# A five-hop graph kernel: first tile multiplied whole in fp32, two pieces of x and the visits of the last hop moved

## What is computed

```python
h = relu(A @ (x @ W1) + b1)
h = relu(A @ (h @ W2) + b2)
x = layernorm(x + h)
f1 = A @ x @ V1
f2 = A @ A @ x @ V2
f3 = A @ A @ A @ x @ V3
out = layernorm(x + (f1 + f2 + f3) / 3.0)
```

## Time and profile before

| | |
|---|---|
| time, median of 3 runs | 254.26 (253.55, 254.26, 254.32) |
| the profiled execution's own time | 253.49 |
| its span (first to last instruction) | 251.7 |
| PE busy | 244.9, 97% of the span |
| DVE busy | 203.2, 81% |
| ACT busy | 192.8, 77% |
| POOL busy | 16.0, 6% |
| chain that ended last | PE 84%, DVE 5%, ACT 3%, issue 3%, DMA 2% |
| split pieces of the ring | 240 on ACT at 629 ns, 240 on DVE at 687 ns |

### The profile page before, as it was taken

The page is one execution under the profiler, slowest core; times in us unless marked ns, Lnnn a source line. Parts: engine busy times, 40 slices in busy tenths (PEclk is TensorE's granted clock), DMA queues, the critical chain, the costliest instruction groups (busy, mean ns, idle before and its releaser), DMA issues.

```text
span 251.7 us, 3740 instructions
## 1 busy us (share of the span) xinstructions
PE 244.9 (97%) x1136; PEld 203.0 (81%) x1136; DVE 203.2 (81%) x395; ACT 192.8 (77%) x335; POOL 16.0 (6%) x23
## 2 busy tenths in 40 slices
PE   8999999999999999999999999999999999999991
PEld 8688888888888888886888888888888888888871
DVE  0998889896789889897888979767676767798865
ACT  2999899886868787978878787777777777779850
POOL 1000000000003021130000000000000000011322
PEclk9999999999999999999999999999999999999999
DMA  6999999930000000000043210000000000301002
GB/s 219 384 390 383 386 386 387 392 133 0 0 3 3 0 0 3 0 0 1 19 105 48 59 25 3 0 0 1 4 0 0 0 0 3 83 1 42 21 24 83
DMA packets 20276, 22.59 MB, mean 90 GB/s; under 512 B 9760, under 2 KB 10656, under 8 KB 20128
## 3 DMA queue, kind: packets, MB, share of 16 engines
q1 hardware_dynamic: 19968, 22.03, 25.5%
q10 hardware_dynamic: 288, 0.33, 0.4%
HBM read 20.25 MB, written 2.10 MB: 89 GB/s over the span
## 4 chain that ended last, share of the span: by engine, by line
PE 84%; DVE 5%; ACT 3%; issue 3%; DMA 2%; SPq 1%; POOL 1%; POOLq 0%; DVEq 0%; ACTq 0%
PE filters L436 18%; PE filters L429 18%; PE filters L430 18%; PE pair L429 9%; PE pair L436 9%; PE pair L430 9%; PE weighted L404 3%; ACT ring_high L572 3%; DVE ring_low L697 2%; DMA adj<-a_t 2%; PE turned L406 1%; DVE stats L613 1%; SPq L293 1%; ACT nodes L533 1%; DVE operand_low L653 0%
## 5 line engine op out<-in xcount | busy, mean ns | idle before, releaser
L697 DVE TENSOR_TENSOR ring_low<-adj,ring_high 128x512 fp32r<-128x512 f32 x240 | 160.1, 687 | 31.4 <-ACT ring_high L572 28.7
L572 ACT ACTIVATE ring_high<-adj 128x512 fp32r<-128x512 f32 x240 | 148.7, 629 | 30.0 <-PE filters L430 14.2
L429 PE MATMUL filters<-ring_high,operand_low 128*128 128x512 f32 x156 | 61.8, 396 | 0.0
L436 PE MATMUL filters<-ring_low,operand_high 128*128 128x512 f32 x156 | 61.0, 391 | 0.2 <-DVE ring_low L697 0.2
L430 PE MATMUL filters<-ring_high,operand_high 128*128 128x512 f32 x156 | 60.8, 389 | 0.0
L436 PEld LDWEIGHTS filters<-ring_low,operand_high 128*128 128x128 f32 x156 | 29.3, 188 | 7.1 <-DVE ring_low L697 0.9
L430 PEld LDWEIGHTS filters<-ring_high,operand_high 128*128 128x128 f32 x156 | 29.3, 188 | 5.7
L429 PEld LDWEIGHTS filters<-ring_high,operand_low 128*128 128x128 f32 x156 | 29.3, 188 | 5.6
L429 PE MATMUL pair<-ring_high,operand_low 128*128 128x512 f32 x84 | 33.3, 396 | 0.0
L436 PE MATMUL pair<-ring_low,operand_high 128*128 128x512 f32 x84 | 32.9, 392 | 0.2 <-DVE ring_low L697 0.2
L430 PE MATMUL pair<-ring_high,operand_high 128*128 128x512 f32 x84 | 32.7, 390 | 0.0
(11 more groups left out here) (86 smaller groups left out, 207.0 us busy)
## 6 DMA issues: line engine op xcount, KB each, us to landing
adj<-a_t SPq DMA_DIRECT2D x48, 256.0 KB, 9.6
resident_raw<-a_t SPq DMA_DIRECT2D x16, 256.0 KB, 9.7
nodes<-x_rows SPq DMA_DIRECT2D x1, 1024.0 KB, 11.8
scratch<-turned_blocks SPq DMA_DIRECT2D x4, 256.0 KB, 2.0
turned_rows<-scratch SPq DMA_DIRECT2D x16, 64.0 KB, 2.5
lead<-lead_in SPq DMA_DIRECT2D x3, 256.0 KB, 4.0
out_rows<-nodes SPq DMA_DIRECT2D x3, 256.0 KB, 2.4
lead<-lead_in ACTq DMA_DIRECT2D x1, 192.0 KB, 2.9
```

The costliest lines, as they stand in the source:

```text
L429: nc.tensor.matmul(bank, y_low, a_high, start=first, stop=False)
L436: used = nc.tensor.matmul(bank, y_high, a_low, start=False, stop=last)
L572: nc.scalar.activation(ring_high[:, n % RING, :], source, ACT.Copy).then_inc(high_ready, 1)
L697: nc.vector.tensor_tensor(ring_low[:, n % RING, :], source, ring_high[:, n % RING, :].bitcast(F32), ALU.subtract).then_inc(low_ready, 1)
```

## The change

There are three parts.

1. **The first tile** (hop 0, chunk 0, tile 0, named `PLAIN`) is no longer split. ACT makes a copy of the first 128 x 128 operand in fp32 (`first_row`), ahead of the high part of x's first group, and PE multiplies it with the raw piece of A in one fp32 product of 512 columns. The high and the low part of this tile on ACT and DVE and its three products go, and all later items of the ring have a number less by one.
2. **`X_SPLIT`**: the splits of x's groups 2 and 3 stand ahead of steps 5 and 9, no longer of 1 and 3. PE still waits for them at tiles 8 and 12.
3. **`POSTS_AFTER`**: in hop 4 the posts, and all that is counted from them, stand one step closer to the end of the chunk: 15 to 14 for chunk 0, 10 to 9 for chunk 1, 5 to 4 for chunk 2.

```diff
-X_SPLIT = (0, 0, 1, 3)
+X_SPLIT = (0, 0, 5, 9)
+PLAIN = (0, 0, 0)
...
-BY_BLOCKS = {(2, 0): 17, (2, 1): 18, (2, 2): 16, (4, 0): 15}
-POSTS_AFTER = {(4, 1): 10, (4, 2): 5, **BY_BLOCKS}
+BY_BLOCKS = {(2, 0): 17, (2, 1): 18, (2, 2): 16, (4, 0): 14}
+POSTS_AFTER = {(4, 1): 9, **BY_BLOCKS}
...
+def in_ring(step):
+    return streamed(step[2]) and step != PLAIN
...
-for _, _, _k in STEPS:
-    BEFORE.append(BEFORE[-1] + streamed(_k))
+for _step in STEPS:
+    BEFORE.append(BEFORE[-1] + in_ring(_step))
...
+            def plain_product():
+                hop, c, k = PLAIN
+                pe.wait_ge(first_row_ready, 1)
+                pe.wait_ge(arrival(c, k), 16)
+                nc.tensor.matmul(sums_of(hop, c), first_row[:], adj[:, c, 0, :], start=True, stop=False)
...
+                if (hop, c, k) == PLAIN:
+                    plain_product()
+                    continue
                 if hop == 0 and c == 0:
                     for g, (first, _) in enumerate(X_GROUPS):
-                        if first == k:
+                        if max(first, 1) == k:
                             pe.wait_ge(operand_low_ready, g + 1)
...
             def x_tiles(g):
                 first, last = X_GROUPS[g]
                 act.wait_ge(first_multiplied, g + 1)
+                if g == 0:
+                    nc.scalar.activation(first_row[:], product_of(g)[:, 0, :], ACT.Copy).then_inc(first_row_ready, 1)
                 nc.scalar.activation(operand_high[:, 0, first:last, :], product_of(g), ACT.Copy
                                      ).then_inc(operand_high_ready, 1)
```

More of the change, by code:

```diff
@@ L163, in graph_layers @@
         turned_blocks = nc.alloc_sbuf_tensor_at("turned_blocks", [P, 2, TILES, D], F32, offset=place[0])
+        first_row = nc.alloc_sbuf_tensor_at("first_row", [P, D], F32, offset=place[0] + TILES * D * 4)
         operand_high = sb("operand_high", [P, 2, TILES, D], F32R)
@@ L191, in graph_layers @@
         first_multiplied = sem("first_multiplied")
+        first_row_ready = sem("first_row_ready")
         x_in = sem("x_in")
@@ L559, in _ @@
                     nc.scalar.activation(lift_high[:], lift_raw[:], ACT.Copy).then_inc(lift_high_ready, 1)
-                if i < STREAMED:
+                if in_ring((hop, c, k)):
                     visits(n)
@@ L573, in _ @@
                     n += 1
-                elif hop == 0:
+                elif i == STREAMED and hop == 0:
                     act.wait_ge(arrival(c, k), 16)
```

## The result

The changed kernel's median is 253.21 us over 17 runs (252.9 to 254.35), the kernel before in the same series 253.83 over 17 (253.3 to 254.32). The ratio is 0.9978 with a 95% interval of 0.997 to 0.9985: 0.56 us less, short of the 0.3% that the prediction took as the least that can be told from no change. So it is **the same** by that bound, though the interval leaves out 1, and inside the range near its low end. Of the 0.59 between 253.21 and the 253.8 forecast, 0.43 is the start of the sum: 254.26 was the median of three runs, that of the 17 is 253.83. The profiled execution took 253.71 (span 251.9) and is one of the changed kernel's slower runs. Why is part of the answer.

A forecast was written before the change was run, and what follows sets the result against it. PE (TensorE), busy 97% of the span, was taken as the bound, so gains come only at start and end: 0.14 + 0.31 = 0.45, from 254.26 to 253.8 us, with an 8-in-10 range of 253.1 to 254.4.

The forecast's parts named there:

- The end, 0.31: Kernel's end: ACT's copy-out no longer waits behind the third chunk's normalising; the adding product starts at 244.90, not 245.21.
- the 1.01 of the working: Third chunk, hop 4: the last variance is ready at 241.94 instead of 242.95.
- Rival 2: End gives nothing: second power over 0.25 later than thought, ACT copies out behind the normalising as before; 254.1, chance 0.13.
- The start, 0.14: First column: DVE's queue sets the pace and PE starts tile 10 at 16.07 instead of 16.21.
- It can start at 8.15, as the first one now: Kernel's start: PE's fp32 product of the first tile begins at 8.15, tile 1 at 9.03.
- the second form of rival 1: Start: DVE never last, PE unbroken from 9.03, tile 10 at 15.24, 0.97 earlier; total 253.0, chance 0.07.
- the forecast's own mechanism: First column: DVE, behind after tile 4, makes seven starts of 0.60; PE waits for its low parts at tiles 5 and 9.
- At most 0.27 passes the second column: Second column: a late load and DVE's low part of its tile 10 let some 0.27 of the start's gain through.
- The sum: Whole kernel: 0.14 at the start and 0.31 at the end give 0.45, below the 0.76 us that can be told.
- rival 1's first form: Start gives all that passes the second column, 0.27, with a first-tile gap of 0.66; total 253.7, chance 0.15.
- Rivals 3: Start slower: DVE's pieces stand 0.68 apart instead of 0.60, and the start costs 0.42; total 254.4, chance 0.03.
- rival 4: Hop 4 slower: a shift ahead of a low part waits for its power until PE runs dry; 254.5, chance 0.05.

The follow-up runs named there:

- before, again: The kernel before, unchanged, run and profiled once more; measured ratio 1.0003 to the kernel before.
- third visits alone: The kernel before with only the third chunk's visits in hop 4 one tile closer (5 to 4); measured ratio 0.9989.
- all visits: The kernel before with only the third part of the change, the visits of hop 4 one tile closer; measured 0.999, -0.25 us.
- both of these: The changed kernel with x's third group split ahead of step 0 and the first chunk's post four steps later; measured ratio 0.9976 to the kernel before.
- x's moves alone: The kernel before with only X_SPLIT = (0, 0, 5, 9), the first tile split as before; measured ratio 0.9994.
- product and moves: The changed kernel with the visits of before, so parts 1 and 2 without part 3; measured 0.9989 against the kernel before, -0.28 us.
- after, again: The changed kernel, unchanged, run and profiled once more; measured ratio 0.9985 to the kernel before.

## Why the prediction was right, and where a term was off

**The end, 0.31: right in mechanism and size.** Measured 1.20 - 0.89 = 0.31, and in every profile with the third chunk's visits moved, changed kernel or not, the copy-out stands 0.04 behind PE's last record and the tail is 7.34 to 7.36, against 0.39 or 0.40 and 7.67 to 7.69 without (nine profiles with, five without; read to the end of the trace, not from the rounded spans of the table). The second power lies beside the last low part and takes 1.00; the normalising is over 0.10 before the copy-out (244.99 - 244.89), where 0.25 was forecast. The 0.15 of margin went with DVE's queue, which moved a little less than forecast: PE's last product starts 2.10 behind the last variance now (244.56 - 242.46), against 1.23 in the earlier trace rows, so the variance gained 0.87 and not the 1.01 of the working. The rule of the Trainium skill cited there, that POOL and VectorE share interfaces ("GPSIMD Engine Reference", section "Specifications"), agrees with the runs: the third chunk's second power takes 1.00 or 1.01 in the nine profiles where it lies beside a low part, and 0.69 in the five where nothing runs on DVE. Rival 2, the end that gives nothing, is out.

**The start, 0.14: the step that failed is "It can start at 8.15, as the first one now".** It took the start of one profiled execution for all. PE's first products run at one of two distances from record to record, 0.21 and then 0.11, and the switch falls anywhere from 4.1 to 7.3 us in 14 profiles. Neither the kernel nor the chip explains it: each of the three series ran on one chip, and within them the switch falls at 4.1 to 7.3, 4.6 to 6.9 and 5.3 to 7.3. With the late switch (x products of 3.2 to 3.4 in the table) the start of before (in "before, again" and "third visits alone") reaches tile 10 at 16.98 and 17.07, with the early one ("before" and "all visits") at 16.21 and 15.97. The changed start doesn't mind: 16.12 and, with both extra edits, 16.14 late, 15.67 to 16.21 otherwise.

The reason can be followed in the rows. After a late switch the fp32 product starts at 9.13; from there PE needs 0.86 and nine tiles of 0.68, 9.13 + 0.86 + 6.12 = 16.11, and 16.12 is what it did. In the repeat of after it is 8.63 + 0.86 + 6.12 = 15.61, and 15.67. PE is the bound there, as in the second form of rival 1, only from a later start. After an early switch DVE is, with its queue behind the loads, as in the forecast's own mechanism: 16.21 with waits where they were forecast. Tile 4's low part is 0.11 ahead of the forecast there (10.68, not 10.79), and seven starts of 0.60 would put tile 9's at 14.88; it stands at 15.14, because tile 8's low part came 0.24 late: ACT had stood 0.26 for tile 7's load and came to tile 8 at 13.19. So the change gives the start nothing or a little at tile 10 in the early case and 0.84 to 0.95 in the late one; of the pieces ahead of tile 3's low part on DVE it takes three away, tile 0's and two of x's.

That the product alone is not enough is seen at tile 10 too: with it x's third and fourth groups still stand ahead of tile 3 (late switch, 16.79, against 16.12 with both). Whether x's moves need the product isn't shown: their one profile had the early switch, and there they reached tile 10 at 15.74 against 16.21 with both.

**"At most 0.27 passes the second column" was right.** PE needs 15.87 from tile 10 to tile 32 when nothing stops it (before, both times). In the repeat of after tile 10 is 0.54 ahead of the first profile of before, tile 32 only 0.17; with the early third group it is 0.35 and 0.17. Against a late start of before (32.85) there is more room, and "both of these", with the late switch, has kept 0.70 of 0.84 at tile 32; the first profile of after, late too, has kept 0.15 of 0.86. Three profiles (after, all visits, x's moves alone) lose 0.54 to 0.92 there. One load of the second column lands late in all 14 profiles; in these three it is that of tile 24, and ACT is idle for 1.23 to 1.36 before it, and only then comes to the posted chunk's piece. Elsewhere it is tile 25 or 26, and ACT waits 0.47 in the earlier trace rows, 0.62 and 0.66 in "product and moves" and "after, again", which lose 0.38 and 0.37. That is why the profile shown above, with the late switch and this load as well, is one of the slower runs of its kernel.

**The sum.** Parts 1 and 2 measured 0.28 us (interval from 0.56 less to 0.03 more), part 3 0.25 to 0.28, both together 0.56 and in the repeat 0.38 (0.9985 of 253.88; the intervals overlap). Forecast 0.45 = 0.14 + 0.31. The start was undersized by about a factor of two if the point estimates are right, which the intervals don't settle; rival 1's first form (0.27) fits the 0.28 of parts 1 and 2 as well as the forecast's 0.14 does. That the sum came so close is in part luck: its 0.14 was worked out for one start, and by the switch alone tile 10 of the kernel before moves more than five times as far. Rivals 3 and 4 are out: DVE's starts stay 0.60 apart (8.78, 9.98 for two pieces), which keeps contradicting the strict reading of the Trainium skill's "VectorE: DVE Perf Modes", section "The DRAIN you can't avoid"; and PE is busy 14.00 of 14.00 us where rival 4 had it run dry.

**What stays open.** The unprofiled runs don't show which switch they had. The two levels of the start fit the scatter of before (17 runs, eight at 253.64 or less, nine at 253.83 or more; its late profile at 254.29, its early one at 253.49), but the runs of it in the three later series fill the space between, and single runs of the changed kernel still reach 254.35 and 254.61. That it gains by being deaf to the switch is shown at tile 10, in profiles, and only argued for the medians. The kernel with x's third group at step 0 has the lowest ratio in both its series, 0.997, 0.76 us less than before. It isn't told apart from the changed kernel.

## What to carry to other kernels

Before a start is costed from one profile, look at a second one of the same kernel: here the two differed by 0.77 us at tile 10, more than the whole change. Where an engine's queue mixes work that waits for a late product with work that doesn't, put the work that waits as far back as its first use allows; here that bought little at tile 10 when the product was early and about 0.85 when it was late, of which later waits left 0.15 in one profile and 0.70 in another. At the end of a kernel ask of each engine whether anything stands between the bound engine's last result and its use; a tile's distance in one number gave here about half of the gain.

## What the runs showed of the hardware

**TensorE's speed at the start of a program varies from run to run.** The busy table of 5 to 7 us, kernel before, first profile and repeat:

```profile
5.00:7.00 2.00, 2.00 (x20) 2.00 (x18) 0.62 (x1) 0.96 (x2) 0.00 (x0) 1.00 1.05 339
```
```profile
5.00:7.00 2.00, 2.00 (x12) 2.00 (x11) 0.22 (x1) 0.60 (x1) 0.00 (x0) 1.00 1.01 370
```

The granted clock reads 1.00 both times, with PE busy throughout and the same work in front of it, but 20 records ran in the one and 12 in the other. PE had been busy since 1.05 in both (its warm-up products). The distances of 0.11 and 0.21 fit the upper and the lower level of the clock (2.4 and 1.2 GHz), which the granted clock of these rows doesn't show. So count records and don't read the start's clock from that column.

**A late load follows a fetch of instructions, in all 14 profiles.** DMA queues of "x's moves alone" from 22.5 to 23:

```profile
q1 hardware_dynamic: 104, 0.19, 103.3%
q8 instruction: 1, 0.02, 13.8%
```

A fetch on the instruction queue takes 13.8% of the 16 engines' time in 0.5 us, so 0.138 x 16 x 0.5 = 1.1 us of one engine, when the loads fill all of them. The same packet of 16 KB is in all 14 profiles, starts between 22.6 and 23.7 and takes 1.09 to 1.13. In each of them the longest gap between two landings of the 64 loads ends 2.2 to 2.6 behind its start: 1.31 to 2.09, where 0.68 is usual. It hits tile 24 in three profiles, tile 25 in nine, and tile 26 in the two where the fetch came last (23.60 and 23.68). So the delay moves with the fetch. That the one makes the other is still argued from the timing; no run took the fetch away, and six profiles have shorter gaps of 1.0 to 1.4 at other places too.
